# Causal softmax attention on one Trainium2 core: where in a step the TensorE queue puts the transposes of the next rows and the second half of the values

## Chip, cores and metric

The kernel runs on one NeuronCore of a Trainium2 chip. The metric is the device time of one execution in microseconds (us); lower is better. Three executions of the kernel before took 2548.25, 2551.59 and 2555.52 us, so their median is 2551.59 us.

## What is computed

Six blocks are applied one after the other to `x` of shape (64, 64, 256), that is 4096 rows of 256 float32: cross attention, a polynomial self attention, a mixture of experts, a second cross attention, causal softmax self attention, and a feed-forward block. The change touches the fifth alone:

```python
qkv = x @ Wqkv.T                                  # x is layer-normed here
q, k, v = jnp.split(qkv, 3, axis=-1)              # 16 heads of 16
dots = jnp.einsum('bhid,bhjd->bhij', q, k) * dh ** (-0.5)
dots = jnp.where(causal_mask, -jnp.inf, dots)     # 64 x 64 for each head
attn = jax.nn.softmax(dots, axis=-1)
out = jnp.einsum('bhij,bhjd->bhid', attn, v).transpose(0, 2, 1, 3).reshape(b, t, d)
x = x + out @ Wout.T + bout
```

## The kernel before

`X`, all rows of `x`, stays in SBUF. Each block of the reference is a phase with its own engine programs and semaphores, and a phase begins only when the one before has ended on all engines. `softmax_attention` (from L969) works on 16 units (`NP`), each of two 128-row tiles, that is four batch elements of 64 rows.

It is a software pipeline written out by hand. In step `s` (0 to 18) four units are in work: `s` (layer norm), `p = s-1` (transposes of the normalised rows, projections to keys, queries and values), `a = s-2` (scores, masking, maximum, exponential, transposes of the weights) and `e = s-3` (product of weights and values, here "attended", then output projection and the addition to `X`). Every engine has its own list of operations for a step and does them in exactly that order. Engines meet only at counting semaphores. Steps 0 to 3 are written out, 4 to 15 are a hardware loop with two steps in its body, 16 to 18 are written out again.

The heads are handled in four groups `j`, each with its PSUM bank `ps_s[j]`. The names that matter:

- TensorE, `step` at L1326: the rows' transposes into `ps_a` (L1334), which wait for `xn_ready` and `q_ready` (the previous unit's queries have been read from `ps_a`); `attended(e, ep, j)` (L1276, products L1289), 16 small products into the two banks `ps_o`; `transposes(a, j)` of the exponentials (L1271), four each, which wait for `exp_ready`; `keys_or_queries` (L1312), for keys into `ps_b`, for queries into `ps_a`; `scores` (L1261), 96 products that complete all four banks together; `values(0)` and `values(1)` (L1319), six products each into `ps_b`; `heads_transposed` (L1298) and `projected_heads` (L1306) into `ps_o`.
- VectorE, `step` at L1112: the low part of the transposed rows, `xT` (L1117); statistics (L1121, L1124); the low part of the keys (L1130); `maximum(a, j)`, masking (L1086) and maximum (L1090); `normalised_heads` (L1094, L1096); the normalised rows `xn` (L1149); the low part of the queries (L1154), which gives `q_ready`; and last in the step `added(e, i)` (L1104), which adds the projection in `ps_o` to `X` and gives `x_updated`.
- ScalarE, `step` at L1207: the high part of `xT` (L1212), the copies `w` of the transposed weights (L1173), the high part of the keys (L1184), the exponentials `prob` (L1168), the high part of the queries (L1226), the copies of the values (L1195, L1199) and of the transposed heads (L1179).
- GpSimd subtracts the maximum (L1071) and adds the bias (L1077). SyncE moves half of the values between partitions by DMA.

Two waits stand next to each other in this story. The products of weights and values overwrite `ps_o`, so the first of them in a step waits for everything that the previous unit had there:

```python
def attended(e, ep, j):
    pe.wait_ge(w_ready, 4 * e + j + 1)
    if j == 0:
        pe.wait_ge(v_ready, e + 1)
        ...
        wait(pe, x_updated, 2 * e)
```

For `e = 0` the value is 0 and `wait` issues nothing. The rows' transposes do not have this wait; theirs is `wait(pe, q_ready, p)`.

Of the kernel before, what the change touches and what calls it, by code (L numbers as in the profile page):

```python
# [86 lines left out]
def wait(eng, sem, value):  # L87

    if isinstance(value, int) and value <= 0:
        return  # L90
    eng.wait_ge(sem, value)


def wait_apart(eng, sem, value, passed):


    eng.wait_ge(sem, value)
    if not isinstance(value, int):
        eng.sem_inc(passed)


def live(t, n=NT):

    return not isinstance(t, int) or 0 <= t < n
# [864 lines left out]
def softmax_attention(nc, c, X, d):  # L969

    NP = NT // 2
    with ExitStack() as ctx:
# [37 lines left out]
        v_done, vs_ready, v_ready = ph.sem("v_done"), ph.sem("vs_ready"), ph.sem("v_ready")  # L1010
# [235 lines left out]
        def _(pe):  # L1246
            def scores(a, ap):

                if isinstance(a, int) and a == 0:
                    pe.wait_ge(cleared, 5)  # L1250
                pe.wait_ge(k_ready, a + 1)
                pe.wait_ge(q_ready, a + 1)
                if live(a - 1, NP):
                    wait_apart(pe, w_ready, 4 * a, passed_pe)
                for i in range(2):
                    for g in range(KC):
                        for n, (b, (x, z)) in enumerate((b, xz) for b in range(2) for xz in THREE_PASSES):
                            for j in range(4):
                                rows = slice(32 * j, 32 * (j + 1))
                                first = (2 * i + g) * P  # L1260
                                mm = nc.tensor.matmul(ps_s[j][:, first:first + P], q2[rows, ap, x, 2 * g + i, :, :]  # L1261
                                                      .rearrange("p b t -> p (b t)")[:, b * P:(b + 1) * P],
                                                      k2[rows, ap, z, g, i, :, b * T:(b + 1) * T],
                                                      start=(n == 0), stop=(n == 5))
                                if i == 1 and g == KC - 1 and n == 5:
                                    mm.then_inc(s_done, 1)

            def transposes(a, j):
                pe.wait_ge(exp_ready, 4 * a + j + 1)
                for n in range(4):  # L1270
                    mm = nc.tensor.transpose(ps_s[j][:, n * P:(n + 1) * P],  # L1271
                                             prob[:, j % 2, 2 * n:2 * n + 2, :].rearrange("p m t -> p (m t)"),
                                             c.ident[:, :])
                mm.then_inc(t_done, 1)
# [5 lines that stand above are left out]
                    if isinstance(e, int):  # L1280
                        wait_apart(pe, v_moved[ep], 64 * (e // 2 + 1), passed_pe)
                    else:
                        wait_apart(pe, v_moved[ep], e * 32 + (64 if ep == 0 else 32), passed_pe)
                    wait(pe, x_updated, 2 * e)
                for i in range(2):
                    for g in range(KC):
                        hh = 4 * g + j
                        for b in range(2):
                            mm = nc.tensor.matmul(ps_o[i][b * T:(b + 1) * T, hh * 2 * D1:(hh + 1) * 2 * D1],  # L1289
                                                  w[:, j, 2 * i + g, b * T:(b + 1) * T],  # L1290
                                                  v[:, ep, i, b, hh, :, :].rearrange("p m d -> p (m d)"),
                                                  start=True, stop=True)
                mm.then_inc(pv_done, 1)

            def heads_transposed(e, i):
                pe.wait_ge(y_ready, 2 * e + i + 1)
                for k in range(KC):
                    mm = nc.tensor.transpose(ps_o[i][:, k * P:(k + 1) * P],  # L1298
                                             y[:, i, :, :].rearrange("p h d -> p (h d)")[:, k * P:(k + 1) * P],
                                             c.ident[:, :])  # L1300
                mm.then_inc(yT_done, 1)

            def projected_heads(e, i):
                pe.wait_ge(yT_ready, 2 * e + i + 1)
                for k in range(KC):
                    mm = nc.tensor.matmul(ps_o[i][:, E:2 * E], yT[:, i, k, :], wo[:, k, :],  # L1306
                                          start=(k == 0), stop=(k == KC - 1))
                mm.then_inc(o_done, 1)

            def keys_or_queries(ps, first, g):  # L1310
                for n, (k, (x, z)) in enumerate((k, xz) for k in range(KC) for xz in THREE_PASSES):
                    mm = nc.tensor.matmul(ps[:, g * 2 * P:(g + 1) * 2 * P],  # L1312
                                          wqkv2[:, x, k, first + g * P:first + (g + 1) * P], xT[:, z, k, :],
                                          start=(n == 0), stop=(n == 3 * KC - 1))
                return mm

            def values(i):
                for n, (k, (x, z)) in enumerate((k, xz) for k in range(KC) for xz in THREE_PASSES):
                    mm = nc.tensor.matmul(ps_b[:, i * E:(i + 1) * E], xT[:, x, k, i * P:(i + 1) * P],  # L1319
                                          wqkv2[:, z, k, 2 * E:3 * E], start=(n == 0), stop=(n == 3 * KC - 1))  # L1320
                return mm
# [4 lines left out]
            def step(s, par):  # L1326
                p, a, e = s - 1, s - 2, s - 3
                pp, ap, ep = 1 - par, par, 1 - par
                if live(p, NP):
                    pe.wait_ge(xn_ready, p + 1)  # L1330
                    wait(pe, q_ready, p)
                    for k in range(KC):
                        for i in range(2):
                            mm = nc.tensor.transpose(ps_a[:, (2 * k + i) * P:(2 * k + i + 1) * P],  # L1334
                                                     xn[:, pp, i, k * P:(k + 1) * P], c.ident[:, :])
                    mm.then_inc(xT_done, 1)
                if live(e, NP):
                    attended(e, ep, 0)
                    attended(e, ep, 1)
                    transposes(e, 3)  # L1340
                if live(p, NP):
                    pe.wait_ge(xT_ready, p + 1)
                    wait(pe, v_ready, p)
                    keys_or_queries(ps_b, E, 0)
                if live(e, NP):
                    attended(e, ep, 2)
                if live(p, NP):
                    keys_or_queries(ps_b, E, 1).then_inc(k_done, 1)
                if live(e, NP):
                    attended(e, ep, 3)  # L1350
                if live(a, NP):
                    scores(a, ap)
                if live(p, NP):
                    keys_or_queries(ps_a, 0, 0)
                    keys_or_queries(ps_a, 0, 1).then_inc(q_done, 1)
                    pe.wait_ge(k_ready, p + 1)
                    values(0)
                if live(a, NP):
                    transposes(a, 0)
                if live(p, NP):  # L1360
                    values(1).then_inc(v_done, 1)
                if live(e, NP):
                    heads_transposed(e, 0)
                    heads_transposed(e, 1)
                if live(a, NP):
                    transposes(a, 1)
                if live(e, NP):
                    projected_heads(e, 0)
                    projected_heads(e, 1)
                if live(a, NP):  # L1370
                    transposes(a, 2)
            tile_steps(pe, step, n=NP, lag=3)


# [1110 lines left out]
```

## Time and profile before

| | before |
|---|---|
| median of three runs | 2551.59 us |
| the profiled execution | 2549.75 us |
| its span in the trace | 2547.8 us |
| TensorE matmuls, busy in the span | 2187.8 us |
| VectorE | 1522.9 us |
| ScalarE | 1073.6 us |
| GpSimd | 1024.0 us |

The profiled execution took 1.95 us more than the span that its trace shows, which is what lies around the first and last instruction. Phase 5, the softmax attention, lies between about 1905 and 2200 us of the span. In a timeline row, the first number is the start, the second the time from the start of the first to the end of the last of the merged instructions; in brackets stands how long the engine had been idle and which instruction released it. Consecutive groups on TensorE overlap a little, so the time from start to start is the one to add up.

### The profile page before, as it was taken

To read this page: it belongs to the slowest core of one execution; us is meant where nothing else is said; L and a number is where in the kernel's file an instruction comes from. 1 tells how busy PE (TensorE), PEld (TensorE's weight loads), DVE (VectorE), ACT (ScalarE), POOL (GpSimd) and SP (SyncE) were. 2 spreads that over 40 slices of the span, in tenths; PEclk is the share of its full clock that TensorE was granted. 3 is DMA by queue.
4 is the path that set the end of the run, shared out by engine and by line. 5 is a ranking of instruction groups with operands and counts; after the bars stand their busy time and mean duration, and the time that the engine had idled before them with its cause. 6 is when DMAs were issued, how large, how long until landed. Compare 5 with 4: busy or idle time off the path is not lost. (4 is left out here: it accounts for less than half of the span.)

```text
span 2547.8 us, 57500 instructions
## 1 busy us (share of the span) xinstructions
PE 2187.8 (86%) x19514; PEld 1607.8 (63%) x19527; DVE 1522.9 (60%) x4179; ACT 1073.6 (42%) x2247; POOL 1024.0 (40%) x1137
## 2 busy tenths in 40 slices
PE   5999999999699989998999999957768888477783
PEld 4888888888599975554555555545547787333332
DVE  4777777777466648751333333346656777477773
ACT  3766666676444422431222222212224555344442
POOL 3444445444100013864555555511123433125555
PEclk9999999999788959999999999989989999698996
DMA  3111000110011030401222222244420000100001
GB/s 126 30 29 37 28 28 28 37 28 19 20 12 10 9 105 3 171 17 56 76 77 78 75 77 78 72 145 165 163 87 10 8 7 9 36 1 1 0 0 66
DMA packets 120797, 128.86 MB, mean 51 GB/s; under 512 B 77697, under 2 KB 95362, under 8 KB 119426
## 3 DMA queue, kind: packets, MB, share of 16 engines
q1 hardware_dynamic: 106450, 89.84, 11.7%
q0 software_dynamic: 13824, 37.77, 4.7%
q8 instruction: 54, 0.88, 0.1%
q14 instruction: 37, 0.30, 0.0%
q10 hardware_dynamic: 432, 0.07, 0.0%
HBM read 96.18 MB, written 27.26 MB: 48 GB/s over the span
## 5 line engine op out<-in xcount | busy, mean ns | idle before, releaser
L1827 PE MATMUL ex_ps_h<-moew_w,ex_xT 128*128 x576 | 286.7, 620 | 20.7 <-DVE ex_xT L1880 9.8
L426 ACT ACTIVATE xa_prob<-xa_neg_s,xa_neg_max 128x256 f32<-128x256 f32 x512 | 224.5, 499 | 140.2 <-DVE xa_neg_max L314 140.2
L1875 DVE TENSOR_TENSOR ex_g<-ex_act_g,ex_ps_h 128x256 f32<-128x256 f32 x144 | 60.7, 422 | 310.6 <-ACT ex_act_g L1860 310.6
L314 DVE CUSTOM_DVE_ANT_0 xa_neg_s<-xa_ps_s,xa_mask 128x256 f32<-128x256 f32 x512 | 191.4, 421 | 36.0 <-PE xa_ps_s L480 21.5
L1804 POOL DMA_INDIRECT ex_xg<-xn_rows,moe_in_row x144 | 139.8, 971 | 158.9 <-PE ex_ps_x L1834 150.4
L1860 ACT ACTIVATE ex_act_g<-ex_ps_h 128x256 f32<-128x256 f32 x144 | 55.3, 384 | 290.3 <-PE ex_ps_h L1827 290.3
L1827 PEld LDWEIGHTS ex_ps_h<-moew_w,ex_xT 128*128 128x128 f32 x576 | 98.0, 190 | 124.0 <-issue 124.0
L509 PEld LDWEIGHTS xa_ps_o<-xa_v,xa_probT 128*64 128x64 f32 x4096 | 140.1, 137 | 47.7 <-issue 42.2
L509 PE MATMUL xa_ps_o<-xa_v,xa_probT 128*64 128x34 f32 x4096 | 168.9, 227 | 0.0
L433 ACT ACTIVATE xa_probT<-xa_ps_s 128x512 f32<-128x512 f32 x256 | 152.0, 594 | 39.6 <-PE xa_ps_s L491 37.1
L1809 POOL DMA_INDIRECT expert_outs<-ex_y,moe_out_row x144 | 142.2, 987 | 63.0 <-ACT ex_y L1864 61.8
L491 PE MATMUL xa_ps_s<-g_ident,xa_prob 128*128 128x128 f32 x1024 | 162.7, 281 | 2.2 <-ACT xa_prob L426 1.6
L1841 PE MATMUL ex_ps_y<-moew_xw,ex_gT 128*128 x576 | 148.4, 380 | 1.2 <-DVE ex_gT L1885 1.2
L2312 PE MATMUL ff_ps_y<-ff_h,ff_tap 128*128 128x512 f32 x256 | 132.0, 642 | 8.0 <-DVE ff_y L2168 7.5
L2115 POOL TENSOR_TENSOR ff_y<-ff_y,ff_scale_b 128x512 f32<-128x512 f32 x64 | 82.1, 1283 | 103.0 <-ACT ff_scale_b L2246 103.0
L491 PEld LDWEIGHTS xa_ps_s<-g_ident,xa_prob 128*128 128x128 f32 x1024 | 111.3, 140 | 10.7 <-ACT xa_prob L426 3.7
L1953 PE MATMUL xb_ps_g<-xb_ctx_rows 128*128 128x256 f32 x512 | 117.8, 384 | 0.0
L1071 POOL TENSOR_TENSOR sa_shifted<-sa_masked,sa_top 128x512 f32<-128x512 f32 x64 | 68.2, 1065 | 123.0 <-DVE sa_top L1090 123.0
L270 POOL TENSOR_TENSOR xa_qz<-xa_q,xa_in_pair 128x256 fp32r<-128x256 f32 x128 | 74.5, 614 | 87.2 <-DVE xa_q L362 87.2
L1841 PEld LDWEIGHTS ex_ps_y<-moew_xw,ex_gT 128*128 128x128 f32 x576 | 98.3, 190 | 9.5 <-issue 2.2
L1953 PEld LDWEIGHTS xb_ps_g<-xb_ctx_rows 128*128 128x128 f32 x512 | 95.9, 192 | 12.6 <-issue 0.4
L1864 ACT ACTIVATE ex_y<-ex_ps_y 128x256 f32<-128x256 f32 x144 | 55.3, 384 | 102.5 <-PE ex_ps_y L1841 102.5
(313 smaller groups left out, 5087.3 us busy)
## 6 DMA issues: line engine op xcount, KB each, us to landing
xa_ctxT<-in_ctxT_dram SPq DMA_DIRECT2D x32, 512.0 KB, 3.7
xb_ctx_rows<-in_ctx_rows_dram SPq DMA_DIRECT2D x32, 512.0 KB, 3.7
xb_expert_y<-expert_outs SPq DMA_DIRECT2D x32, 512.0 KB, 4.5
moew_w<-in_moe_w_dram SPq DMA_DIRECT2D x8, 1024.0 KB, 13.2
g_x<-in_x_dram SPq DMA_DIRECT2D x4, 1024.0 KB, 10.0
sa_v<-sa_vs SPq DMA_DIRECT2D x128, 32.0 KB, 2.2
xn_rows<-rs_xn SPq DMA_DIRECT2D x8, 512.0 KB, 2.9
moew_xw<-in_moe_w_dram SPq DMA_DIRECT2D x8, 512.0 KB, 5.5
```

What stands on the lines that cost most here:

```text
L314: ins = nc.vector.tensor_tensor_reduce(neg_s[:, u % 2, g, :], ps_s[j][:, g * S:(g + 1) * S], mask[:, b, :], -1.0, 3e38, ALU.add, ALU.min, ...
L426: ins = nc.scalar.activation(prob[:, u % 2, i, :], neg_s[:, u % 2, i, :], ACT.Exp, bias=neg_max[:, u % 2, i:i + 1], scale=-1.0)
L433: nc.scalar.activation(probT[:, u % 2, :, :, :].rearrange("p i c t -> p (i c t)"), ps_s[u % 4][:, :], ACT.Copy).then_inc(t_ready, 1)
L491: mm = nc.tensor.transpose(ps_s[u % 4][:, k:k + P], prob[:, u % 2, g, ch * P:(ch + 1) * P], c.ident[:, :])
L509: mm = nc.tensor.matmul(ps_o[b][rows, q * 2 * D1:(q + 1) * 2 * D1], probT[:, u % 2, g, ch, rows], v[:, ap, 2 * b + ch, 2 * q:2 * q + 2, :] ...
L1804: nc.gpsimd.indirect_dma_start(xg[:, s % 4, :], None, rows, bass.IndirectOffsetOnAxis(ap=c.in_row[:, s:s + 1], axis=0)).then_inc(x_loaded[ ...
L1809: nc.gpsimd.indirect_dma_start(c.y_dram[:, :], bass.IndirectOffsetOnAxis(ap=c.out_row[:, e:e + 1], axis=0), y[:, e % 4, :], None).then_inc ...
L1827: mm = nc.tensor.matmul(ps_h[1 - par][:, :], xT[:, 1 - par, k, :], c.w1[:, own, k, :], start=(k == 0), stop=(k == KC - 1))
L1841: mm = nc.tensor.matmul(ps_y[1 - par][:, 0:E], gT[:, 1 - par, k, :], c.w2[:, own, k, :], start=(k == 0), stop=(k == KC - 1))
L1953: mm = nc.tensor.matmul(ps_g[q % 2][b][:, g * E:(g + 1) * E], ctx_rows[:, q, 2 * b + k, g * P:(g + 1) * P], ctx_rows[:, q, 2 * b + k, :], ...
L2115: nc.gpsimd.tensor_tensor(y[:, gp, j, :], y[:, gp, j, :], scale_b[:, gp, :], ALU.mult)\
L2312: mm = nc.tensor.matmul(ps_y[j % 2][:, :], tap[:, i, j, :], h[:, j % 4, :, 2 * i:2 * i + T], start=(i == 0), stop=(i == 1))
```

## The change

On TensorE alone, two operations of a step change places. `attended(e, ep, 0)` and `attended(e, ep, 1)` come first in a step, ahead of the rows' transposes and of the waits of these. `values(1)` follows `values(0)` at once, ahead of `transposes(a, 0)`. No instruction is added or removed, and the other engines' lists stay as they are.

```diff
             def step(s, par):
                 p, a, e = s - 1, s - 2, s - 3
                 pp, ap, ep = 1 - par, par, 1 - par
+                if live(e, NP):
+                    attended(e, ep, 0)
+                    attended(e, ep, 1)
                 if live(p, NP):
                     pe.wait_ge(xn_ready, p + 1)
                     wait(pe, q_ready, p)
...
                                                      xn[:, pp, i, k * P:(k + 1) * P], c.ident[:, :])
                     mm.then_inc(xT_done, 1)
                 if live(e, NP):
-                    attended(e, ep, 0)
-                    attended(e, ep, 1)
                     transposes(e, 3)
                 if live(p, NP):
                     pe.wait_ge(xT_ready, p + 1)
...
                     pe.wait_ge(k_ready, p + 1)
                     values(0)
+                    values(1).then_inc(v_done, 1)
                 if live(a, NP):
                     transposes(a, 0)
-                if live(p, NP):
-                    values(1).then_inc(v_done, 1)
                 if live(e, NP):
                     heads_transposed(e, 0)
```

## Rows read from the trace of the kernel before

**Rows 1.** The page, busy time, share of the span and instructions of each engine

```profile
PE 2187.8 (86%) x19514; PEld 1607.8 (63%) x19527; DVE 1522.9 (60%) x4179; ACT 1073.6 (42%) x2247; POOL 1024.0 (40%) x1137
```

**Rows 2.** Waits in the stage: engine, line, releaser, us in total, times, longest

```profile
PE sa_ps_s L1271 <- ACT sa_prob L1168: 22.4, 18, 3.3
...
PE sa_ps_a L1334 <- DVE sa_q L1154: 9.6, 14, 0.8
...
PEld sa_ps_o L1289 <- DVE g_x L1104: 2.5, 12, 0.2
```

**Rows 3.** Timeline of TensorE (start us, us, engine, line), one steady step

```profile
2052.75 0.66 PE L1334 MATMUL sa_ps_a<-g_ident,sa_xn 128*128 128x128 f32 x4 [0.64 <-DVE sa_q L1154]
2053.41 1.13 PE L1289 MATMUL sa_ps_o<-sa_v,sa_w 128*64 128x34 f32 x32
2054.46 0.66 PE L1271 MATMUL sa_ps_s<-g_ident,sa_prob 128*128 128x128 f32 x4
2054.88 0.95 PE L1312 MATMUL sa_ps_b<-sa_xT,sa_wqkv 128*128 128x256 f32 x6
...
2057.84 2.90 PE L1261 MATMUL sa_ps_s<-sa_k,sa_q 32*128 32x128 f32 x96
...
2062.21 0.87 PE L1319 MATMUL sa_ps_b<-sa_wqkv,sa_xT 128*128 128x256 f32 x6
2064.28 0.66 PE L1271 MATMUL sa_ps_s<-g_ident,sa_prob 128*128 128x128 f32 x4 [1.20 <-ACT sa_prob L1168]
2064.69 0.95 PE L1319 MATMUL sa_ps_b<-sa_wqkv,sa_xT 128*128 128x256 f32 x6
...
2068.25 0.60 PE L1271 MATMUL sa_ps_s<-g_ident,sa_prob 128*128 128x128 f32 x4
2069.59 0.63 PE L1334 MATMUL sa_ps_a<-g_ident,sa_xn 128*128 128x128 f32 x4 [0.74 <-DVE sa_q L1154]
```

**Rows 4.** Timeline of VectorE, the same step

```profile
2052.62 0.74 DVE L1104 TENSOR_TENSOR g_x<-g_x,sa_ps_o 128x256 f32 x2
2054.07 0.69 DVE L1117 TENSOR_TENSOR sa_xT<-sa_ps_a,sa_xT 128x512 fp32r<-128x512 f32 x1 [0.72 <-ACT sa_xT L1212]
...
2060.86 0.69 DVE L1086 TENSOR_TENSOR sa_masked<-sa_ps_s,sa_mask 128x512 f32<-128x512 f32 x1 [0.24 <-PE sa_ps_s L1261]
...
2068.77 0.68 DVE L1154 SCALAR_TENSOR_TENSOR sa_q<-sa_ps_a,sa_q 128x512 fp32r<-128x512 f32 x1
2069.37 0.73 DVE L1104 TENSOR_TENSOR g_x<-g_x,sa_ps_o 128x256 f32 x2
```

**Rows 5.** Timeline of ScalarE, the same step

```profile
2053.44 0.60 ACT L1212 ACTIVATE sa_xT<-sa_ps_a 128x512 fp32r<-128x512 f32 x1
...
2063.60 0.63 ACT L1168 ACTIVATE sa_prob<-sa_shifted 128x512 f32<-128x512 f32 x1 [4.67 <-POOL sa_shifted L1071]
```

**Rows 6.** Timeline of TensorE, the keys of step 3

```profile
1937.59 0.99 PE L1312 MATMUL sa_ps_b<-sa_xT,sa_wqkv 128*128 128x256 f32 x6 [0.18 <-DVE sa_xT L1117]
```

**Rows 7.** Timeline of VectorE, step 3

```profile
1936.85 0.69 DVE L1117 TENSOR_TENSOR sa_xT<-sa_ps_a,sa_xT 128x512 fp32r<-128x512 f32 x1 [1.85 <-ACT sa_xT L1212]
...
1943.52 0.69 DVE L1086 TENSOR_TENSOR sa_masked<-sa_ps_s,sa_mask 128x512 f32<-128x512 f32 x1 [0.15 <-PE sa_ps_s L1261]
```

**Rows 8.** Timeline of TensorE, the rows' transposes of steps 4 and 16

```profile
1952.16 0.65 PE L1334 MATMUL sa_ps_a<-g_ident,sa_xn 128*128 128x128 f32 x4 [0.85 <-DVE sa_q L1154]
...
2153.44 0.63 PE L1334 MATMUL sa_ps_a<-g_ident,sa_xn 128*128 128x128 f32 x4 [0.72 <-DVE sa_q L1154]
```

**Rows 9.** Busy time by stretch: length, engines' busy us, granted clock, DMA share, GB/s

```profile
1925.00:1942.00 17.00, 13.93 (x256) 12.27 (x251) 10.63 (x21) 9.32 (x20) 6.62 (x8) 1.00 0.09 9
...
2053.00:2070.00 17.00, 15.06 (x232) 13.52 (x230) 12.56 (x28) 9.35 (x20) 6.86 (x10) 1.00 0.09 9
```

**Rows 10.** The same for TensorE alone, one stretch at the stage's end

```profile
2160.00:2180.00 20.00, 15.17 (x269) 0.92 0.07 9
```

**Rows 11.** Timeline of TensorE, the rows' transposes of step 1

```profile
1909.56 1.09 PE L1334 MATMUL sa_ps_a<-g_ident,sa_xn 128*128 128x128 f32 x4 [15.66 <-DVE sa_xn L1149]
```

## The prediction, made before the changed kernel had run

> **What bounds the kernel now.** I read the page first. Over the whole span TensorE is the busiest engine, with 2187.8 of 2547.8 us [rows 1]. That is a mean over six phases. The change touches one phase of 295 us, so the question is what limits a step there.
>
> The waits of that stage come next. TensorE waits in three places that the change touches [rows 2]: for the exponentials (22.4 us in 18 waits), for the queries' low part ahead of the rows' transposes (9.6 us in 14), and, a little, for the addition to `X` ahead of the products of weights and values (2.5 us in 12, seen on the weight loads). The third row is small only because the rows' transposes stand in front of it in the queue and fill that time.
>
> Then the timelines of a steady step. The rows' transposes begin at 2052.75 and again at 2069.59 [rows 3]; from step 4 to step 16 they repeat twelve times in 2153.44 - 1952.16 = 201.28 us, so a step takes 16.77 us [rows 8]. What closes that circle is seen by going backwards from a wait:
> - The transposes at 2069.59 were released by the queries' low part on VectorE, which ended at 2068.77 + 0.68 = 2069.45 [rows 3, 4].
> - From 2060.86, its first masking, to 2069.37 + 0.73 = 2070.10, the end of the addition, VectorE has no wait: 9.24 us in one piece. The row at 2060.86 shows the wait that starts it: 0.24 us for the scores [rows 4].
> - The scores come at the end of a piece of TensorE without a gap, from the transposes at 2052.75 over products, keys and scores (2057.84 + 2.90 = 2060.74) [rows 3].
>
> So a step is bound by a ring, half on TensorE (8.0 us) and half on VectorE (8.6 us to the queries' end), not by the busy time of either. The 1.20 us gap on TensorE ahead of the exponentials' transposes at 2064.28 [rows 3] lies outside of the ring: those transposes wait for an exponential that ended at 2063.60 + 0.63 = 2064.23 [rows 5], and this one was waiting for GpSimd and VectorE. A faster TensorE at this place finds the exponentials no earlier.
>
> **Part 1, the second half of the values goes ahead of the exponentials' transposes.** Six products, whose successor starts some 0.8 us after them; they take 0.95 us by themselves [rows 3]. The first half starts at 2062.21 and takes 0.87 us, so both end at about 2064.0, before the exponential is there at 2064.23. The transposes keep their place, and what stands behind the second half (transposed heads, next exponentials, projection) may start up to 0.8 us earlier. Nothing in the ring asks for those: the addition on VectorE at 2069.37 follows the queries without a wait [rows 4]. TensorE would be finished earlier and wait longer for VectorE. Price: 0, at most a few hundredths. The cover is the 1.20 us gap; without it the exponentials would come up to 0.95 us later.
>
> **Part 2, two products of weights and values go ahead of the rows' transposes.** These 32 instructions now stand first, with their wait for the addition to `X`. That wait ends with the second addition, at 2053.36 in the first of the two steps (2052.62 + 0.74), and the products followed it there at 2053.41 [rows 3, 4]. The transposes were already done by then: they had run from 2052.75, in that very wait. Now they are behind it, and behind 1.05 us of products (2054.46 - 2053.41), so they start at 2054.46 instead of 2052.75, 1.71 us late.
>
> Who waits for them: ScalarE's high part follows their start by 0.69 us (2053.44), VectorE's low part follows that by 0.63 us (2054.07) [rows 3 to 5], and the keys follow that by 0.74 us where they did wait for it (1936.85 to 1937.59) [rows 6, 7]. Together 2.06 us from the transposes to the keys. Before, this was covered by the two products and by the last exponentials' transposes, and the keys started at 2054.88, 2.13 us after the transposes, with 0.07 us to spare. Now only the exponentials' transposes are left as cover, 0.42 us from start to start [rows 3]. The keys, and the scores behind them, come later by 1.71 - 0.07 = 1.64 us.
>
> The new ring, from rows: 9.24 (VectorE, first masking to the end of the addition) + 0.05 (to the products) + 1.05 (the products) + 0.69 + 0.63 + 0.74 (to the keys) + 5.93 (keys to the first masking, 1937.59 to 1943.52 [rows 6, 7]) = 18.33 us. Against 16.77 that is 1.56 us a step. The difference to 1.64 is the 5.93 of step 3 where the steady step has 5.98. I take 1.56.
>
> How many steps: a step pays if it has both a unit to transpose and one to attend, and an addition before it. Those are steps 4 to 16, 13 of them. Step 3 has no addition to wait for (the wait of unit 0 is empty), and there the products can run in the wait for the queries; I give it 0, between 0 and 1.6. Steps 17 and 18 have no rows to transpose, step 2 has nothing to attend. No DMA is moved: SyncE waits for copies of the values that ScalarE makes in its own order.
>
> Bounds of a step's price: 1.05 us, if the addition's wait had been over earlier and only the products stood in the way; and 2.0 us, if TensorE needs up to 0.4 us more to get going after its two new waits. For 0.4 no row here has the case itself; it is more than half of the 0.64 us that the old wait lasted [rows 3], which I take as the most that could hide in it.
>
> **Sum.** 13 x 1.56 = 20.3 us. The profiled execution took 2549.75 us, its span 2547.8; with the sum it is 2570.0. The median of the runs is 1.8 above the profiled execution, so I forecast 2572 for a median. The bounds give 13 x 1.05 = 13.7 and 13 x 2.0 = 26, that is 2563 to 2578, or 2580 with 1.6 for step 3. A change of under 0.3% (7.7 us) can't be told from none here.
>
> **Rivals.**
>
> *A, TensorE is the bound, and the change fills its gap.* Then the 1.20 us gap goes in 14 steps (3 to 16), 16.8 us, less what remains of it (1.20 - 0.80 = 0.40 a step, 5.6 us) at the cautious end: faster by 11 to 17 us, 2535 to 2540. For it: 86% busy over the span [rows 1], and 15.06 of 17 us in a steady step [rows 9]. Against it: in each of those steps TensorE waits 0.64 to 0.85 us for the queries [rows 3, 8], so time won at the gap only makes that wait longer. It decides if the first masking on VectorE comes sooner than 16.77 us after the last one. Chance 0.07.
>
> The Trainium skill speaks for A. "Perfetto Trace Analysis", under Identifying Performance Opportunities, says to take the most contended engine and find what blocks it in its gaps. By that, closing the largest repeating gap of TensorE should pay; the ring above says that this gap isn't on the path, and I go with the rows.
>
> *B, the wait for the addition is over when the products come up.* The transposes of the third exponentials start at 2068.25 [rows 3]; the two products would follow from about 2068.7 and end near 2069.8, in the present wait for the queries (0.74 us), and the rows' transposes would go 0 to 0.2 us late. This is the change doing well what it does: 14 x 0 to 0.2 = 0 to 3 us, 2552 to 2555, no difference. Against it: the addition ends at 2070.10, after the queries' part (2069.45), in VectorE's fixed order [rows 4], and the twelve small waits on it [rows 2]. It holds only if the addition is moved up, which nothing does. Chance 0.07.
>
> *C, the ring grows and TensorE's clock falls too.* With 18.33 us a step TensorE is busy 15.06 x 16.77 / 17 = 14.9 us of it, 81%. The stretch from 1925 to 1942 had 13.93 of 17, 82%, at a granted clock of 1.00; the one from 2160 to 2180 had 15.17 of 20, 76%, and 0.92 [rows 9, 10]. At the stage's start, after 15.66 us without work, the same four transposes took 1.09 us, 1.65 times the 0.66 of the steady step [rows 3, 11]. If a third of the 13 steps ran so, their 7.6 us of TensorE in the ring (1.05, 0.66, 5.93) would grow by 0.65 x 7.6 = 4.9 us each, 21 us in all: 2593. The row with nearly the same share at full clock speaks against it. Chance 0.06.
>
> The Trainium skill, "Perfetto Trace Analysis", under Matmul Optimizations, says that the engine scales with its use and that products should run back to back in batches; by that the two new waits could cost clock, which is C.
>
> **Chances.** Forecast 0.80, A 0.07, B 0.07, C 0.06. Slower by over 0.3%: forecast and C, 0.86. Within 0.3%: B, 0.07. Faster: A, 0.07. The range goes from 2562, just under the low bound, to 2586: the bound of 2580 and a C in which some steps alone lose clock. The likeliest case lies in it whole.
>
> **What the changed profile would show.** The step from one start of L1334 to the next goes from 16.77 to about 18.3 us. L1289 waits for L1104 in 13 steps with about 1.5 us on TensorE, and the wait of L1334 for L1154 is gone. The keys (L1312) wait for the low part of the rows (L1117) by 0.8 to 0.9 us in each. The wait of L1271 for L1168 is 0.3 us in place of 1.20 at the first exponentials. VectorE waits near 2.3 us instead of 0.72 ahead of L1117, and stays in one piece from the first masking to the addition. The granted clock stays at 1.00. The forecast is wrong if L1289 finds the addition done, if VectorE's piece of 9.24 us gets shorter or breaks up, or if the step is under 17.5 us.

## The result and the profile after

The changed kernel took 2588.25 us (median of five runs, 2587.58 to 2589.84), 1.0147 times the kernel before (95% interval 1.0133 to 1.0161). It is slower, as forecast, but by 37 us and not by 20, which is outside of the range of 2562 to 2586. Its profiled execution took 2587.79 us, 38.0 more than that before.

Busy times on the page:

```profile
PE 2213.0 (86%) x19514; PEld 1629.0 (63%) x19527; DVE 1522.4 (59%) x4179; ACT 1069.5 (41%) x2247; POOL 1022.9 (40%) x1137
```

Against [rows 1], TensorE alone is busy for longer, by 25 us, with as many instructions: some of its work ran slower. The waits of the stage (columns as in [rows 2]):

```profile
PEld sa_ps_o L1289 <- DVE g_x L1104: 17.7, 12, 1.7
PE sa_ps_o L1289 <- DVE g_x L1104: 16.9, 15, 1.6
...
PE sa_ps_b L1312 <- DVE sa_xT L1117: 15.6, 16, 1.9
...
PE sa_ps_s L1271 <- ACT sa_prob L1168: 9.7, 14, 3.3
```

The wait for the queries' part is gone. In its place stand the one for the addition and a new one for the keys. A steady step of the new TensorE order, in the timeline:

```profile
2066.24 0.63 PE L1271 MATMUL sa_ps_s<-g_ident,sa_prob 128*128 128x128 f32 x4
2068.38 1.13 PE L1289 MATMUL sa_ps_o<-sa_v,sa_w 128*64 128x34 f32 x32 [1.51 <-DVE g_x L1104]
2069.44 0.66 PE L1337 MATMUL sa_ps_a<-g_ident,sa_xn 128*128 128x128 f32 x4
2069.93 0.60 PE L1271 MATMUL sa_ps_s<-g_ident,sa_prob 128*128 128x128 f32 x4
2071.51 0.99 PE L1312 MATMUL sa_ps_b<-sa_xT,sa_wqkv 128*128 128x256 f32 x6 [0.97 <-DVE sa_xT L1117]
...
2080.94 0.66 PE L1271 MATMUL sa_ps_s<-g_ident,sa_prob 128*128 128x128 f32 x4 [0.50 <-ACT sa_prob L1168]
...
2087.88 0.66 PE L1337 MATMUL sa_ps_a<-g_ident,sa_xn 128*128 128x128 f32 x4
```

Set against [rows 3], the wait for the queries' part (0.74) has become 1.51 us for the addition and 0.97 us for the rows' low part. The wait for the exponential is 0.50 in place of 1.20. The step takes 18.44 us. VectorE, ahead of and in the same step:

```profile
2052.32 0.69 DVE L1117 TENSOR_TENSOR sa_xT<-sa_ps_a,sa_xT 128x512 fp32r<-128x512 f32 x1 [2.43 <-ACT sa_xT L1212]
...
2059.08 0.69 DVE L1086 TENSOR_TENSOR sa_masked<-sa_ps_s,sa_mask 128x512 f32<-128x512 f32 x1 [0.24 <-PE sa_ps_s L1261]
...
2067.59 0.73 DVE L1104 TENSOR_TENSOR g_x<-g_x,sa_ps_o 128x256 f32 x2
```

From the first masking to the end of the addition it is 9.24 us in one piece, as in [rows 4], and it now waits 2.43 us for the rows. This much was forecast. A second loss shows in the busy times by stretch, from one start of the rows' transposes to the next (columns as in [rows 9]):

```profile
1991.03:2009.45 18.42, 15.28 (x231) 13.30 (x228) 12.31 (x26) 8.84 (x19) 6.61 (x8) 1.00 0.07 7
2009.45:2032.56 23.11, 22.14 (x232) 20.26 (x229) 12.31 (x26) 8.90 (x19) 6.61 (x8) 0.63 0.04 4
2032.56:2051.00 18.44, 15.35 (x232) 13.35 (x229) 12.31 (x26) 8.84 (x19) 6.61 (x8) 1.00 0.08 9
2087.88:2110.98 23.10, 22.11 (x232) 20.23 (x229) 12.31 (x26) 8.90 (x19) 6.62 (x8) 0.63 0.04 4
2129.41:2152.97 23.56, 22.18 (x233) 20.31 (x229) 12.31 (x26) 8.91 (x19) 6.61 (x8) 0.64 0.05 5
```

Of the twelve stretches from step 4 to step 16, nine take 18.4 to 18.5 us at a granted clock of 1.00, and three take 23.1 to 23.6 at 0.63 to 0.64. Before, all twelve were at 1.00. The timeline shows such a step from within:

```profile
2008.40 1.13 PE L1289 MATMUL sa_ps_o<-sa_v,sa_w 128*64 128x34 f32 x32 [1.51 <-DVE g_x L1104]
2009.45 0.66 PE L1337 MATMUL sa_ps_a<-g_ident,sa_xn 128*128 128x128 f32 x4
2009.95 1.02 PE L1271 MATMUL sa_ps_s<-g_ident,sa_prob 128*128 128x128 f32 x4
2011.52 1.65 PE L1312 MATMUL sa_ps_b<-sa_xT,sa_wqkv 128*128 128x256 f32 x6 [0.56 <-DVE sa_xT L1117]
...
2016.70 5.39 PE L1261 MATMUL sa_ps_s<-sa_k,sa_q 32*128 32x128 f32 x96
...
2027.19 0.60 PE L1271 MATMUL sa_ps_s<-g_ident,sa_prob 128*128 128x128 f32 x4
```

The products and the rows' transposes right behind the 1.51 us gap still take their 1.13 and 0.66 us; from 2009.95 on the same work takes up to 1.86 times as long (the scores 5.39 us where they took 2.90). So the clock goes from 2.4 to 1.2 GHz within 2 us behind the gap, and it stays there for 17 us. VectorE waits for these scores:

```profile
2022.20 0.69 DVE L1086 TENSOR_TENSOR sa_masked<-sa_ps_s,sa_mask 128x512 f32<-128x512 f32 x1 [3.15 <-PE sa_ps_s L1261]
```

From the keys to the first masking it is 10.68 us here and 6.01 in a step at full clock (2053.07 to 2059.08). That is the whole loss of the step, 4.67 us; what still runs slowly behind the scores is covered by VectorE's 9.24 us.

**Where the 38.0 us are.** Between the rows' transposes of steps 1 and 16 the trace after has 284.41 us, the one before 243.88: 40.5 more. Everything before that was 4.0 us shorter in this execution and everything behind it 1.5 us longer. The 40.5 are 34.5 from step 4 to 16 (235.75 against 201.28), of which 14.5 is what the three slow stretches have over 18.44 and 20.0 the longer ring, and 6.1 before step 4. Of these last, some 3 us are a low clock in step 2: from its transposes to those of step 3 it is 18.89 us at 0.71, and 15.82 at 1.00 with the same order of the products in a later run (the second one with the attended products alone). The values alone brought such a step 2 as well (17.70 us at 0.71, against 15.25 before). The rest is 0.6 us for the new order in that stretch, 1.3 in the next (18.34 against 17.02) and 1.1 in step 1, which differed by about as much between two executions of one kernel (11.32 and 10.32 in the two profiles with the attended products alone).

### The profile page after: what moved, and what is told of

It reads as the page before. It is cut to its first block and busy times, and to the rows that moved or that the text cites. A ratio compares the mean times of both kernels' runs of the same rounds, so it can differ in the third digit from the quotient of the medians.

```text
span 2585.8 us, 57500 instructions
## 1 busy us (share of the span) xinstructions
PE 2213.0 (86%) x19514; PEld 1629.0 (63%) x19527; DVE 1522.4 (59%) x4179; ACT 1069.5 (41%) x2247; POOL 1022.9 (40%) x1137
```

## The experiments

The first two runs separate the two parts, the third moves the addition, and the others are on the clock, on the price of the wait, and on a shorter ring.

**The values alone.** On TensorE, of the kernel before:

```diff
                     values(0)
+                    values(1).then_inc(v_done, 1)
                 if live(a, NP):
                     transposes(a, 0)
-                if live(p, NP):
-                    values(1).then_inc(v_done, 1)
```

> The kernel before with the second half of the values ahead of the exponentials' transposes, and nothing else. Theory (the products of weights and values ahead of the rows' transposes make the whole loss): no difference, a steady step of 16.77 us, the wait for the exponential at 0.3 to 0.5 us instead of 1.20, the wait for the queries' part about 0.2 longer, 2549 to 2554 us. Rival (the joined values take part in the loss, as the work in one piece leaves a longer gap behind it): 5 to 15 us slower, with a granted clock under 1.00 in some steps.

Measured: 2549.97 us against 2548.53 for the kernel before, measured beside it, ratio 1.0006 (0.9995 to 1.0017), steps of 16.68 to 16.86 us at a clock of 1.00. The two waits changed as expected, in the list of waits of this kernel:

```profile
PE sa_ps_a L1334 <- DVE sa_q L1154: 11.7, 13, 0.9
PE sa_ps_s L1271 <- ACT sa_prob L1168: 11.1, 17, 3.3
```

11.3 us came off the second and 2.1 went onto the first [rows 2]; of the rest, TensorE is counted as busy for some 0.35 us a step more (15.2 against 14.9). Part 1 alone makes no difference that stands clear of the noise, which here goes up to 4 us. The sign that the rival named is there in one place: step 2 has a clock of 0.71 in this profile and takes 2.5 us longer than before.

**The attended products alone.** The other half of the change:

```diff
+                if live(e, NP):
+                    attended(e, ep, 0)
+                    attended(e, ep, 1)
                 if live(p, NP):
                     pe.wait_ge(xn_ready, p + 1)
...
                 if live(e, NP):
-                    attended(e, ep, 0)
-                    attended(e, ep, 1)
                     transposes(e, 3)
```

> The kernel before with the two products of weights and values ahead of the rows' transposes, and nothing else. Theory: a step of 18.4 us at full clock, so 20 to 22 us from 13 steps; how many steps run at the low clock is open, 0 to 4 at 4.7 to 5.1 us each, so 2572 to 2592. If the joined values have no part in the clock, it is 2588 as with the whole change, with about three slow steps; if their gap has, it is near 2573 with none.

Measured: 2569.22 us, ratio 1.0081 (1.0064 to 1.0097). All steps from 3 to 16 at a clock of 1.00:

```profile
2011.80:2030.23 18.43, 14.96 (x233) 13.43 (x229) 12.31 (x26) 8.95 (x19) 6.62 (x8) 1.00 0.07 7
```

So part 2 alone gives the forecast's ring and its 20 us. The other 16 to 19 us (by the ratios, or from one median to the other) need both parts.

**The addition first.** The changed kernel, with this on VectorE:

```diff
                     ins.then_inc(xn_ready, 1)
+                if live(e, NP):
+                    for i in range(2):
+                        added(e, i)
                 if live(p, NP):
                     dve.wait_ge(q_high, p + 1)
...
-                if live(e, NP):
-                    for i in range(2):
-                        added(e, i)
```

> The changed kernel, and on VectorE the addition to X goes ahead of the queries' low part, so that the first products of weights and values are released 0.6 us sooner. Theory (the ring goes from the first masking over the addition to these products): a step at full clock is 18.44 - 0.6 = 17.8 us, 13 x 0.6 = 8 us less at equal clock, 2580, and less still if fewer steps run at the low clock. Rival (the rows' transposes and the queries' part set the ring, not the addition): the step stays at 18.4 us.

Measured: 2563.81 us, ratio 1.0067 (1.005 to 1.0083). The step is 17.83 us, 0.61 shorter, in every stretch from 4 to 16, and none is at the low clock:

```profile
2022.00:2039.82 17.82, 15.28 (x232) 13.30 (x229) 12.31 (x26) 8.84 (x19) 6.63 (x8) 1.00 0.07 7
```

And in its timeline:

```profile
2056.59 1.13 PE L1289 MATMUL sa_ps_o<-sa_v,sa_w 128*64 128x34 f32 x32 [0.91 <-DVE g_x L1104]
```

The addition is in the ring, as the theory said. TensorE's gap ahead of the products is 0.91 us here, and the time is 16 us under the 2580 of equal clock, about what three slow steps cost.

**Both gaps filled.** The changed kernel with repeated transposes, whose result is the same:

```diff
-                for n in range(4):
+                for n in [0, 1, 2, 3] * (1, 1, 4, 3)[j]:
```

> The changed kernel with idle time of TensorE filled by work whose result is the same: the transposes of the third exponentials are issued four times in place of once, those of the fourth three times, some 1.3 and 0.8 us a step. Theory (the low clock in three of the steps comes from TensorE's idle time in each): the granted clock is 1.00 in all steps from 3 to 16, each takes 18.4 to 18.6 us, and the time falls by about 14 us to 2574. Rival (those three steps are slow for another reason): 2588 or more, with three steps of 23 us.

Measured: every step from 3 to 16 at 1.00 and 18.33 to 18.53 us, 267.03 us between the transposes of steps 1 and 16 in place of 284.41, so 17.4 less. The whole kernel took 2578.97, only 9 less than 2588: in this profile the part before step 1 is 4.0 us longer than after the change alone, and the part behind step 16 is 4.1 us longer, nearly all of it in steps 17 and 18, where the repeated work is done too. What the filling did to the clock is read from the stretches.

**Each gap by itself.** `(1, 1, 4, 1)[j]` fills the one ahead of the addition, `(1, 1, 1, 3)[j]` the one ahead of the keys.

> The changed kernel with the transposes of the third exponentials issued four times in place of once (1.3 us of TensorE ahead of the wait for the addition), the gap ahead of the keys left as it is. Theory (the low clock needs the two gaps one soon after the other, 1.51 and 0.97 us with 2.2 us of work between): no step from 3 to 16 at the low clock, steps of 18.4 us, 2570 to 2579. Rival (each gap is enough): some steps at the low clock, over 2580.

> The changed kernel with the transposes of the fourth exponentials issued three times (0.8 us of TensorE ahead of the wait for the keys), the gap ahead of the addition left as it is. Theory (both gaps together are needed): no step from 3 to 16 at the low clock, steps of 18.4 us, 2570 to 2579. Rival (the 1.51 us gap alone does it): two to four steps of 23 us, over 2582.

Measured: 2572.09 us with the first filled, and no step from 3 to 16 under 1.00. With the second filled 2577.59 us; four of the twelve stretches have a clock of 0.91 and 19.6 to 19.7 us. One of these:

```profile
2008.55 1.13 PE L1289 MATMUL sa_ps_o<-sa_v,sa_w 128*64 128x34 f32 x32 [1.51 <-DVE g_x L1104]
2009.61 0.71 PE L1337 MATMUL sa_ps_a<-g_ident,sa_xn 128*128 128x128 f32 x4
2010.12 2.76 PE L1271 MATMUL sa_ps_s<-g_ident,sa_prob 128*128 128x128 f32 x12
2012.53 1.38 PE L1312 MATMUL sa_ps_b<-sa_xT,sa_wqkv 128*128 128x256 f32 x6
2013.84 0.66 PE L1289 MATMUL sa_ps_o<-sa_v,sa_w 128*64 128x34 f32 x16
```

Neither theory had this. The first gap alone brings the clock down, but with work and no pause behind it the clock is back after about 4 us (products of 0.66 at 2013.84) and the step loses 1.25 us. In the changed kernel, with the second gap, it stays down for 17 us and the step loses 4.7 to 5.1.

**The wait without the products.** The order of before:

```diff
                     wait(pe, q_ready, p)
+                    if live(e, NP):
+                        wait(pe, x_updated, 2 * e)
```

> The kernel before, in its own order, with one wait added: the rows' transposes also wait for the addition to X. It prices the wait apart from the products. Theory: the transposes start 0.65 us later, the products still cover most of the chain to the keys, so a step takes 9.24 + 0.05 + 2.1 + 5.93 = 17.3 us, 0.55 more than 16.77; 13 x 0.55 = 7 us slower, 2555 to 2558. Rival (the wait is the whole loss): a step of 18.4 us, 20 us slower.

Measured: 2560.76 us against 2548.08, ratio 1.0045 (1.0028 to 1.0062); 12.7 us, of which the ring explains its part: a step at full clock is 17.37, 0.60 more. The remainder is clock. Three of the 13 stretches from step 3 on are at 0.91 and lose about 1.4 us each. Two of them lie behind a gap of 1.29 us; in the third, step 3, the clock fell behind waits of 1.21 and 0.40 us with four transposes between them, which the kernel before has in the same place at full clock. One of the two, and the stretch behind it:

```profile
1986.99:2005.81 18.82, 16.32 (x228) 14.74 (x229) 12.31 (x26) 9.14 (x20) 6.60 (x9) 0.91 0.07 7
2005.81:2023.18 17.37, 14.84 (x228) 13.38 (x229) 12.31 (x26) 9.06 (x20) 6.62 (x9) 1.00 0.07 8
```

**A longer gap.** The changed kernel, with this on VectorE ahead of the addition:

```diff
                                                    ALU.mult, ALU.subtract).then_inc(q_ready, 1)
+                    nc.vector.tensor_tensor(spare[:, :], wqkv[:, 0, 0:2 * E], wqkv[:, 1, 0:2 * E], ALU.add)
```

> The changed kernel with one more instruction of about 0.6 us on VectorE, between the queries' low part and the addition (a sum into a tile that nobody reads), so that TensorE's first gap grows from 1.51 to about 2.1 us. Theory (more idle time close together gives more steps at the low clock): a full-clock step of 19.0 us, 8 us more, and more than three slow steps, at least 5: over 2606. Rival (which steps are slow does not depend on the gap): 8 us more and three slow steps, 2596.

Measured: 2612.23 us, ratio 1.0243. The added instruction costs 0.87 us a step, more than the 0.6 expected, and the gap is 2.39 us. The shortest step has 19.30 us (18.44 + 0.87), but seven of the twelve stretches take 22.2 to 24.5 us at a clock of 0.62 to 0.81. More steps fall with the longer gap, as the theory said. In two of the seven the clock was back after about 7 us, although the second pause is there:

```profile
2085.99 1.25 PE L1291 MATMUL sa_ps_o<-sa_v,sa_w 128*64 128x34 f32 x32 [2.38 <-DVE g_x L1105]
2089.70 1.65 PE L1314 MATMUL sa_ps_b<-sa_xT,sa_wqkv 128*128 128x256 f32 x6 [0.56 <-DVE sa_xT L1118]
2093.81 0.66 PE L1291 MATMUL sa_ps_o<-sa_v,sa_w 128*64 128x34 f32 x16
```

In the other five it stayed down for about 17 us.

**Once more, side by side.** The changed kernel and the one with the attended products alone, on one chip.

> The changed kernel once more, on the same chip as the next one. Theory (the low-clock steps belong to this order of work and come back in every execution, at places that the start of the stage shifts): 2586 to 2592, three steps of 23 us in the profile, perhaps others than before. Rival (the three slow steps were an accident of one profiled execution): fewer of them, and times spread down to 2574.

> The kernel with the two products of weights and values ahead of the rows' transposes and nothing else, once more, beside the changed kernel on one chip. Theory (without the joined values no step falls to the low clock): 13 steps of 18.4 us at a granted clock of 1.00, 2568 to 2575, and 15 to 20 us less than the changed kernel in the same rounds. Rival (its clean profile was an accident): slow steps here too and a spread of times up to 2588.

Measured: 2583.51 us (2575.52 to 2589.93) and 2568.18 (2564.27 to 2574.8), 15.3 apart. The changed kernel's profile has three slow stretches again, two of them at other steps than the first time; the other's has none:

```profile
2007.53:2030.63 23.10, 22.12 (x232) 20.25 (x229) 12.31 (x26) 8.90 (x19) 6.61 (x8) 0.63 0.04 4
2049.06:2072.62 23.56, 22.16 (x232) 20.28 (x229) 12.31 (x26) 8.90 (x19) 6.61 (x8) 0.64 0.05 5
2164.77:2188.14 23.37, 22.16 (x232) 20.31 (x229) 12.31 (x26) 8.90 (x19) 6.62 (x8) 0.63 0.05 5
```

So the slow steps are no accident of one execution. Their places are, and their number probably too: the execution of 2575.52 us, which has no profile, had a mean clock of 0.935 where the profiled one had 0.929, so the theory's 2586 to 2592 for every execution was too narrow. Between the transposes of steps 1 and 16 the two profiles differ by 17.7 us: 14.7 are the three slow steps, and 3.0 the low clock in step 2. That the joined values matter is shown by this pair and by the first two runs. How they do is not: their order makes the gap ahead of the addition 1.51 in place of 1.30 us, but a gap of 1.29 was enough in the run with the wait alone.

**A shorter ring.** The values are joined, and on VectorE:

```diff
                     ins.then_inc(var_ready, 1)
+                    dve.wait_ge(rstd_ready, s + 1)
+                    wait(dve, xT_done, s - 1)
+                    for i in range(2):
+                        ins = nc.vector.tensor_scalar(xn[:, par, i, :], X[:, 2 * s + i, :], mv[:, par, i, 0:1],
+                                                      rstd[:, par, 1, i:i + 1], ALU.subtract, ALU.mult)
+                    ins.then_inc(xn_ready, 1)
```

(and the same lines go from behind the maxima). The first of the two kernels here has this alone, the second a move on ScalarE beside it.

> The kernel before with the values joined, and on VectorE the normalised rows moved from behind the maxima to right behind the statistics, into the 3.2 us wait for the high keys. It takes 1.4 us out of VectorE's side of the ring. Theory (the ring has a second branch: ScalarE works without a pause from the first exponential at 2063.60 to the high part of the rows at 2070.26, which was as late as TensorE's side): almost nothing is won, a step stays at 16.5 to 16.8 us, 2545 to 2552. Rival (VectorE's piece alone closes the ring): a step of 15.7 to 16.0 us, 10 to 14 us faster.

> As the run before it, and on ScalarE the last exponential and the copy of the third transposed weights go behind the high part of the rows of the next step, with the fourth exponentials' transposes on TensorE behind the first half of the keys. It takes 1.1 us out of ScalarE's branch as well. Theory (the ring of a step runs over VectorE, ScalarE and TensorE, and gets shorter when all three do): a step of 15.6 to 15.9 us at full clock, 11 to 15 us faster than before, 2534 to 2541. Rival (another wait takes its place, such as the output projection for the addition): 16.3 us or more.

Measured: 2548.89 us for the first, ratio 1.0006 (0.9995 to 1.0017), with steps of 16.57 and 16.74 us. The rows' transposes are over at 2046.28, and ScalarE, without a wait, comes to the rows' high part (L1211 here) 0.9 us later:

```profile
2045.63 0.65 PE L1333 MATMUL sa_ps_a<-g_ident,sa_xn 128*128 128x128 f32 x4
```

```profile
2046.68 0.62 ACT L1167 ACTIVATE sa_prob<-sa_shifted 128x512 f32<-128x512 f32 x1
2047.20 0.59 ACT L1211 ACTIVATE sa_xT<-sa_ps_a 128x512 fp32r<-128x512 f32 x1
```

The second kernel has also this on ScalarE, and on TensorE `transposes(e, 3)` goes behind the first half of the keys:

```diff
                 if live(e, NP):
+                    probabilities(e, 3)
+                    transposed(e, 2)
                     transposed(e, 3)
...
-                if live(a, NP):
-                    transposed(a, 2)
-                    probabilities(a, 3)
```

It took 2542.45 us against 2548.3, ratio 0.9969 (0.9956 to 0.9982), in ten runs: faster than both kernels, if little. The step is 16.15 us, not 15.6 to 15.9. The rows' transposes no longer wait for VectorE, but stand behind those of the third exponentials. These come right behind ScalarE's exponential, which ends at 2047.97 and had waited for GpSimd, and right behind the projection on TensorE, which leaves no pause either:

```profile
2047.34 0.63 ACT L1167 ACTIVATE sa_prob<-sa_shifted 128x512 f32<-128x512 f32 x1 [0.41 <-POOL sa_shifted L1071]
```

```profile
2046.22 1.99 PE L1304 MATMUL sa_ps_o<-sa_wo,sa_yT 128*128 128x256 f32 x8
2048.05 0.63 PE L1269 MATMUL sa_ps_s<-g_ident,sa_prob 128*128 128x128 f32 x4
2048.59 0.65 PE L1332 MATMUL sa_ps_a<-g_ident,sa_xn 128*128 128x128 f32 x4
```

So something else did take the place, as the rival said, if with a step shorter than its 16.3. Which of the exponential and the projection has to come sooner, or whether both have to, was not tried.

## Why the prediction was wrong, point by point

**What bounds a step.** Right, with one piece missing. The ring over VectorE and TensorE is confirmed by three runs that changed one piece of it each: 0.61 us off for the addition moved up, 0.60 on for the wait alone, 0.87 on for an instruction of 0.87. The missing piece is ScalarE's branch, as late as the other; it changed nothing in the sum. That it is why the normalised rows moved early won nothing is read from the rows, and borne out by the last run, in which the step got shorter once ScalarE's list was changed too.

**Part 1, the values: 0.** Right by themselves (1.0006). Wrong as a term of the whole change: with part 2 they bring the low clock, 15 to 19 us.

**Part 2, the ring: 1.56 us a step.** Measured 1.66 (18.43 to 18.44 against 16.77), 0.10 under-sized, nearly all of it in the last term: from the keys to the first masking it is 6.01 us (2053.07 to 2059.08), where I took step 3's 5.93. 13 steps of 1.56 gave 20.3, and the runs with part 2 alone measured 20.7 and 19.9. Step 3, put at 0, took 0.6 (15.82 against 15.25), and the first of the 13 took 1.3. The lower bound of 2563 left out the 1.8 us from the profiled execution to the median; with them it is 2565, which changes nothing here.

**The clock.** This is the step that failed: the sum has no term for the clock. "The granted clock stays at 1.00" was taken from a stretch with 82% busy that had been at 1.00, so rival C, the only one with a price for it, got a chance of 0.06. Measured, the clock cost 15 to 19 us: three slow steps (14.5 us) and step 2 (some 3 us). The mean busy share of a step does not decide it. In the changed kernel stretches with 15.3 of 18.4 us (83%) are at full clock, and the same stretch falls to 0.63 at another time; the kernel with part 2 alone has less (14.95 of 18.43, 81%) and not one slow step in 24, the one with the wait alone has more (14.85 of 17.37, 85%) and two in twelve. What starts the fall is the pause at the head of the step: filled or cut to 0.91 us, it brings none. It is not its length alone, as 1.29 to 1.31 us gave both outcomes.

C was nearer than my forecast (2593 against 2588), in part by luck. It had a third of 13 steps slow, against three of twelve, and 4.9 us a slow step, against 4.7 to 5.1. But it stretched products, transposes and the time from the keys to the masking by 1.65 each; in two of the three measured steps only that time grew, by 1.78 (from 6.01 to 10.68 us), and in none were the two products at the head of the step slowed.

**A and B.** Both out. In A the gap at the exponentials was closed from 1.20 to 0.50 us and nothing got faster; in B the addition was to be over in time, and it was 1.51 us late. The Trainium skill's rule to find what blocks the most contended engine in its gaps ("Perfetto Trace Analysis", Identifying Performance Opportunities), taken as A takes it, gives the wrong place here: the largest repeating gap of the busiest engine wasn't on the ring. The same page of the Trainium skill says to run matmuls back to back in batches (Matmul Optimizations), and the missing 15 to 19 us agree with that: they came with pauses of 1.51 and 0.56 to 0.97 us and went when the first was filled.

## What to carry to other kernels

In a hand-ordered pipeline, find the ring that closes a step, going backwards through the waits over all engines, and look at what stands ahead of the instruction that closes it. A wait moved to the head of a queue is paid by all that follows it, and here the transposes had used just that wait. A pause on TensorE is priced twice, once as a pause and once as a risk for the clock of the work behind it, so look at how long each new pause is and how soon the next one follows, and not at the busy share of the step alone.

## What the runs showed of the hardware

TensorE fell from 2.4 to 1.2 GHz within a stage in which it was over 80% busy, behind pauses of 1.29 and 1.51 us, and only in two to four of twelve steps; behind 2.27 to 2.40 us in seven. Behind 0.91 us (12 steps) and 0.20 us (24) it stayed up, and also in the 24 steps with 1.30 us and the values apart. The way back went with what followed: about 4 us where the work came in one piece (six steps of two kernels), and where a second pause of 0.56 to 0.64 us came first, 17 us in eleven steps and 7 us in two. One fall, in step 3 of the run with the wait alone, came behind no pause longer than 1.21 us. The Trainium skill, "TensorE: Matmul & The Clock Gate", section "A second HAM failure mode: psum-queue depth-cycling", describes another kernel, in which short idle times between groups of matmuls make the clock swing between its two levels; these runs agree, with their 4.7 us a step.

What decides in which steps the clock falls stays open. So does step 2: its stretch was at 0.71 to 0.73 in six profiles, all with the values joined, and at 0.96 to 1.00 in the four with the values apart; of the other four with the values joined, two were at 0.86 to 0.88 and two (both gaps filled, rows early) at 1.00.
